# The second mixture of a two-layer decoder: rows and results scattered to their slots, tiles and results loaded plainly

## The chip, the cores and the metric

The kernel runs on one core of a Trainium2 chip. The metric is the device time of one execution in microseconds (us). Before the change three runs took 1368.06, 1368.84 and 1370.04 us; the median is 1368.84 us.

## The reference

A decoder of two layers on x of 4 x 256 tokens with 256 channels. Each layer adds three blocks to x, each on a layer norm of x: in layer 0 a recurrent mix, a cross attention to 1601 context rows and a mixture of 8 experts; in layer 1 an attention with 16 heads, a cross attention to the first 256 context rows, and a second mixture. The change is about that last block:

```python
logits = flat @ router_w.T                            # 1024 tokens x 16 experts
_, topk_idx = jax.lax.top_k(logits + router_bias, 2)
w = softmax scores of the two chosen experts, divided by their sum
for e in range(16):
    out += combine[:, e:e+1] * ((silu(flat @ Wu[e]) * (flat @ Wg[e])) @ Wd[e])
out += (silu(flat @ Su) * (flat @ Sg)) @ Sd           # shared expert
```

## The kernel before

The kernel is written engine by engine: one instruction stream each for TensorE (PE), ScalarE (ACT), the vector engine (DVE), GpSimd (POOL) and SyncE (SP), with semaphores written out by hand between them. Each engine runs its stream in order, so a wait holds all that stands behind it on that engine. Matrix products go through eight PSUM banks that are handed out in turn (`PsumBanks`): a product counts up `filled`, and the engine that reads the bank counts up `emptied`. The five phases are divided by `ended`, at which all engines meet; the second mixture is the end of phase 5.

X holds the 1024 tokens as 8 tiles of 128 tokens x 256 channels, and HN[5] their layer norm. In the second mixture every token has two choices, so there are 2048 rows of work. They are sorted by expert into slots, with each expert's count rounded up to whole tiles of 128 slots: 31 tiles (`TILES1`) always suffice. Slots without a token are padding.

1. Front. SyncE stores HN[5] to DRAM as `token_rows` (xs1, L2300 to L2303). TensorE computes the logits, the shared expert's hidden values (`shared_up`) and a count by expert (`rank1`). The vector engine picks the two experts of each token and works out the slot of each choice, `e_idx` (L1938, 128 x 16: 128 tokens, 2 choices x 8 tiles). The inverse list, the token in each slot, it makes with one-hot matrices `e_A` and `e_B` (L1942 to L1947), which TensorE multiplies (`tile_tokens`, L1085); L1954 to L1956 turn that into `e_ids`. `e_eid` (L1951) says which expert each tile has; TensorE loads it into registers. TensorE also computes the first half of the shared expert's output (`shared_down`, 4 of 8 token tiles), which the vector engine adds to X.
2. Tile loop. GpSimd gathers the rows of tile j from `token_rows` by `e_ids` (an indirect DMA of 128 rows of 1 KB, L2180), up to eight tiles ahead (`e_x` has eight buffers). TensorE turns the tile (`rows_turned`, L1094), multiplies it with the expert's up and gate weights (`tile_up`), turns the gated hidden values (`hidden_turned`) and multiplies them with the down weights (`tile_down`); the four steps of neighbouring tiles are interleaved (L1139 to L1147). ScalarE and the vector engine move and gate what lies between. ScalarE copies the result to one of four buffers `e_y` (L1453 to L1457), and SyncE stores it in slot order to DRAM as `tile_results` (ys1, L2304 to L2306).
3. Tail. TensorE computes the other half of the shared output. When all 31 stores have landed, GpSimd gathers for each token tile the rows of the first and of the second choices (L2183 to L2185, 16 indirect DMAs into `e_yg`). The vector engine works out the weights `e_w` (L1983 to L1987) and adds each weighted row tile to X (L1991, L1993), and SyncE stores X as the output (L2307 to L2309).

GpSimd's indirect DMAs are issued by its own instructions, on its own queue; SyncE's plain DMAs go to another queue.

Of the kernel before, what the change touches and what calls it, by code (L numbers as in the profile page):

```python
# [13 lines left out]
P = 128  # L14
# [72 lines left out]
def decoder(nc, x, ctx_512, L0_attn_Wk, L0_attn_Wv, L0_attn_Wr, L0_attn_Wo, L0_attn_time_decay, L0_attn_time_first,  # L87
# [5 lines left out]
    with ExitStack() as ctx:  # L93
# [5 lines left out]
        def sem(name):  # L99
            return ctx.enter_context(nc.semaphore(name))  # L100
# [209 lines left out]
        xs1 = nc.dram_tensor("token_rows_6", [B * T, C], F32, kind="Internal").ap()  # L310
        ys1 = nc.dram_tensor("tile_results_6", [TILES1 * P, C], F32, kind="Internal").ap()
# [39 lines left out]
        xs1_stored = sem("token_rows_stored")  # L351
# [9 lines left out]
        both_added = sem("both_results_added")  # L361
# [145 lines left out]
        def _(pe):  # L507
# [623 lines left out]
            tile_tokens()  # L1131
            pe.wait_ge(*banks.emptied(("sg", 1)))
            for t in range(4):
                shared_down(t)
# [13 lines left out]
            pe.wait_ge(*banks.emptied(("sg", 3)))  # L1148
            for t in range(4, NT):
                shared_down(t)  # L1150
# [4 lines left out]
        def _(act):  # L1155
# [311 lines left out]
            nc.scalar.activation(f_e[:, :, :], f_e[:, :, :], ACT.Exp).then_inc(e_exp, 1)  # L1467
            ended(act, 5)
# [3 lines left out]
        def _(dve):  # L1472
# [465 lines left out]
            link(V.tensor_copy(e_idx[:, :], slot))  # L1938
# [4 lines left out]
            V.tensor_scalar(e_A[:, :, 0, :], e_one[:, :, :], e_p, None, ALU.mult)  # L1943
            V.tensor_tensor(e_A[:, :, 1, :], e_one[:, :, :], bcast(e_high, 32), ALU.mult)
            for k in range(2):
                V.tensor_tensor(e_B[:, NT * k:NT * (k + 1), :], bcast(e_q[:, NT * k:NT * (k + 1)], P),
                                e_iota.unsqueeze(1).to_broadcast([P, NT, P]), ALU.is_equal).then_inc(onehot_ready, 1)  # L1947
            link(V.tensor_tensor(e_past[:, :, :], e_end[:, 0:E1 - 1].unsqueeze(1).to_broadcast([P, 32, E1 - 1]),
                                 bcast(e_j, E1 - 1), ALU.is_le))
            link(V.tensor_reduce(e_ef[:, :], e_past[:, :, :], AX, ALU.add))  # L1950
            V.tensor_copy(e_eid[:, :], e_ef[:, :]).then_inc(eid_ready, 1)  # L1951
# [28 lines left out]
            for t in range(4, NT):  # L1980
                residual(("sd", t), t)
# [5 lines left out]
            link(V.tensor_tensor(e_w[:, :, :], e_s[:, :, :], e_sum[:, :].unsqueeze(1).to_broadcast([P, 2, NT]), ALU.mult))  # L1987
# [10 lines left out]
        def _(pool):  # L1998
# [191 lines left out]
        def _(sp):  # L2190
# [79 lines left out]
            sp.dma_start(s_mask[:, :], mask_c).then_inc(masks_loaded, 16)  # L2270
            sp.wait_ge(*banks.filled(("a", "o", len(A_UNITS) - 1)))
# [28 lines left out]
            for g in range(2):  # L2300
                sp.wait_ge(hn_ready, NT * 5 + 4 * (g + 1))
                sp.dma_start(xs1[4 * g * P:4 * (g + 1) * P, :].rearrange("(t p) c -> p t c", p=P),
                             HN[5][:, 4 * g:4 * (g + 1), :]).then_inc(xs1_stored, 16)  # L2303
# [9 lines left out]
def shape_constants():  # L2313
# [3 lines left out]
    def angles(n, dim, base):  # L2317
# [23 lines left out]
        row(P * np.tile(np.arange(NT), 2)), row(P * np.arange(8)), row(np.tile(np.arange(NT) > 0, E1)), tri - 1], axis=1)  # L2341
# [40 lines left out]
```

## Time and profile before

| what | value |
|---|---|
| median of three runs | 1368.84 us |
| span of the profiled execution, first to last instruction | 1379.6 us |
| TensorE busy | 1272.7 us (92%) |
| vector engine busy | 868.2 us (63%) |
| GpSimd busy | 824.0 us (60%) |
| ScalarE busy | 634.6 us (46%) |
| mean granted clock of TensorE | 0.954 of full |

The profiled execution's own time is known here by its span. The profile gives, for one execution, every instruction with its start and length; times are us from the first instruction. An instruction of a shared helper has the helper's line (L515 is every matmul, L523 every turning, L1167 every ScalarE copy), so the tile names tell them apart. "PE idle before, <-X" names what released the engine.

### The profile page before, as it was taken

Reading aid. Unit: us, or ns where it says so; the run is one execution under the profiler, and the core shown is the slowest. Engines: PE = TensorE matmul, PEld = TensorE weight load, DVE = VectorE, ACT = ScalarE, POOL = GpSimd, SP = SyncE. Lnnn points to the kernel's source line nnn. Section 1 sums busy time; section 2 is a strip of 40 time slices with the busy share of each in tenths; the row PEclk is TensorE's granted clock in tenths of the full one; section 3 lists DMA queues with packets and bytes.
Section 4 is the critical chain, followed back from the end, with each engine's and each line's share of the span. In section 5 each row is a group of like instructions: output and inputs, shape, how many; then the busy total and the mean of one; then the engine's idle time right before and its main releaser. Section 6 shows DMA issues by size and latency. Waiting matters only on the chain.

```text
span 1379.6 us, 20358 instructions
## 1 busy us (share of the span) xinstructions
PE 1272.7 (92%) x7123; PEld 826.8 (60%) x7123; DVE 868.2 (63%) x1490; ACT 634.6 (46%) x1687; POOL 824.0 (60%) x748
## 2 busy tenths in 40 slices
PE   7999997999999999999999758998999999989792
PEld 4865554666666666666668643445776874556582
DVE  4756666677777777778865636675666123664443
ACT  3731123445554455544551416887665115872151
POOL 1267005799999999999993445887444004560444
PEclk9999997999999999999999888999999997998897
DMA  9501111000000000000005620000000105200263
GB/s 261 134 9 32 37 31 27 9 8 9 9 11 10 9 9 9 10 11 9 9 5 176 195 65 2 1 1 1 1 1 1 27 1 155 63 1 32 69 142 118
DMA packets 66172, 58.91 MB, mean 43 GB/s; under 512 B 19424, under 2 KB 62968, under 8 KB 65560
## 3 DMA queue, kind: packets, MB, share of 16 engines
q1 hardware_dynamic: 62952, 49.09, 12.7%
q0 software_dynamic: 3120, 8.52, 2.6%
q8 instruction: 58, 0.95, 0.3%
q14 instruction: 42, 0.34, 0.1%
HBM read 40.69 MB, written 8.52 MB: 36 GB/s over the span
## 4 chain that ended last, share of the span: by engine, by line
PE 79%; DVE 6%; ACT 5%; POOL 4%; issue 4%; DMA 1%; DVEq 0%; SPq 0%; POOLq 0%; ACTq 0%
PE PS L515 73%; PE PS L523 5%; ACT s_sc L1402 2%; POOL a_m L2137 2%; POOL a_m L2131 2%; DVE s_mx L1859 1%; ACT a_m L1356 1%; DVE pm L1622 1%; DVE HN L1504 0%; PE PS L729 0%; DMA f_xg<-token_rows,f_ids 0%; POOL s_sc L2152 0%; PE PS L685 0%; POOL f_xg L2119 0%; PE PS L623 0%
## 5 line engine op out<-in xcount | busy, mean ns | idle before, releaser
L2080 POOL TENSOR_TENSOR PWS<-PWS 128x1024 f32<-128x1024 f32 x160 | 379.7, 2373 | 45.1 <-ACT PWS L1286 25.8
L1622 DVE TENSOR_REDUCE pm<-PS 128x2 f32<-128x1024 f32 x192 | 225.8, 1218 | 69.3 <-PE PS L515 68.7
L1286 ACT ACTIVATE PWS<-PS 128x512 f32<-128x512 f32 (+1 forms) x416 | 213.3, 599 | 78.4 <-PE PS L515 78.2
L515 PE MATMUL PS<-PWS,KVR 128*64 128x256 f32 (+1 forms) x1664 | 185.8, 380 | 0.0
L515 PE MATMUL PS<-QALL,KH 128*128 128x512 f32 (+1 forms) x416 | 182.6, 439 | 0.9 <-DVE QM L1646 0.9
L515 PE MATMUL PS<-QM,KL 68*128 68x512 f32 (+1 forms) x416 | 167.3, 402 | 0.0
L2152 POOL TENSOR_SCALAR s_sc<-s_sc,s_ri 128x128 f32<-128x128 f32 (+1 forms) x256 | 104.5, 429 | 98.9 <-DVE s_ri L1866 98.9
L515 PEld LDWEIGHTS PS<-PWS,KVR 128*64 128x64 f32 (+1 forms) x1664 | 121.4, 137 | 59.0 <-issue 0.9
L515 PEld LDWEIGHTS PS<-QALL,KH 128*128 128x128 f32 (+1 forms) x416 | 77.9, 187 | 76.9 <-ACT PWS L1286 57.4
L1402 ACT ACTIVATE s_sc<-PS,s_nb 128x128 f32<-128x128 f32 (+1 forms) x256 | 104.5, 433 | 3.9 <-DVE s_nb L1862 3.9
L1859 DVE TENSOR_REDUCE s_mx<-PS 128x2 f32<-128x512 f32 (+2 forms) x112 | 65.7, 611 | 50.1 <-PE PS L515 50.0
L515 PE MATMUL PS<-KH,QALL 64*128 64x512 f32 (+1 forms) x512 | 89.3, 408 | 7.0 <-DVE pm L1622 7.0
L515 PE MATMUL PS<-a_wT,HT 128*128 128x512 f32 x192 | 93.4, 620 | 0.7 <-issue 0.7
L1297 ACT ACTIVATE QALL<-CTX 128x256 fp32r<-128x256 f32 x32 | 13.3, 417 | 154.0 <-DVE CTX L1659 154.0
L515 PEld LDWEIGHTS PS<-QM,KL 68*128 68x128 f32 (+1 forms) x416 | 79.0, 190 | 6.2
L515 PEld LDWEIGHTS PS<-KH,QALL 64*128 64x128 f32 (+1 forms) x512 | 46.9, 189 | 43.7 <-issue 26.0
L515 PE MATMUL PS<-z_HTh,z_w 128*128 128x512 f32 x192 | 67.5, 420 | 2.4 <-DVEq L502 2.4
L2180 POOL DMA_INDIRECT e_x<-token_rows,e_ids x31 | 29.5, 951 | 67.2 <-DVE e_ids L1956 46.8
L2131 POOL TENSOR_TENSOR a_m<-a_m,a_m 128x512 f32<-128x512 f32 x40 | 51.0, 1276 | 29.5 <-DVE a_m L1836 29.5
L1271 ACT ACTIVATE QALL<-PS 64x512 fp32r<-64x512 f32 x32 | 19.0, 594 | 106.3 <-PE PS L515 105.9
L1525 DVE TENSOR_TENSOR X<-X,PS 128x256 f32<-128x256 f32 x40 | 16.8, 419 | 76.8 <-PE PS L515 76.7
L1390 ACT ACTIVATE s_pt<-PS 128x512 f32<-128x512 f32 x64 | 38.5, 602 | 53.6 <-PE PS L523 53.6
(328 smaller groups left out, 2518.3 us busy)
## 6 DMA issues: line engine op xcount, KB each, us to landing
QALL<-qlo SPq DMA_DIRECT2D x32, 128.0 KB, 2.4
QM<-QALL SPq DMA_DIRECT2D x64, 64.0 KB, 2.0
f_w<-in_L_ffn_w_dram SPq DMA_DIRECT2D x2, 2048.0 KB
tile_results<-e_y SPq DMA_DIRECT2D x31, 128.0 KB
a_nat<-in_L_attn_w_qkv_dram SPq DMA_DIRECT2D x1, 3072.0 KB, 13.0
x_wq<-in_L_xattn_Wq_dram SPq DMA_DIRECT2D x1, 2048.0 KB, 10.4
x_wo<-in_L_xattn_Wo_dram SPq DMA_DIRECT2D x2, 1024.0 KB, 6.9
a_wo<-in_L_attn_w_o_dram SPq DMA_DIRECT2D x1, 2048.0 KB, 17.5
```

What stands on the lines that cost most here:

```text
L515: return nc.tensor.matmul(o, a, b, start=start, stop=stop, **kw)
L523: last = nc.tensor.transpose(ps[0:w, c:c + r], a, ident[0:r, 0:r])
L1286: nc.scalar.activation(PW[c][0:rows, j * HALF:(j + 1) * HALF], st_bank("block", LT * u + lt)[0:rows, :], ACT.Exp).then_inc(p_ready, 1)
L1390: nc.scalar.activation(s_pt[:, m % 2, 0, :], ps, ACT.Copy).then_inc(emptied["act_turned"], 1)
L1402: ins = nc.scalar.activation(s_sc[:, k % 4, h, 0:nk], ps[:, j * nk:(j + 1) * nk], ACT.Exp, bias=s_nb[:, k % 3, h:h + 1], scale=scale, accu ...
L1622: V.tensor_reduce(pm[u % 2][:, :, i // 3, i % 3], src, AX, ALU.max).then_inc(nat_read, 1)
L1859: ins = V.tensor_reduce(s_mx[:, k % 3, i * per:(i + 1) * per], banks.bank(key)[:, 0:per * nk].rearrange("p (h k) -> p h k", h=per), AX, AL ...
L2080: G.tensor_tensor(ACC[:, :], PW[0][:, :] if i == 0 else ACC[:, :], PW[i + 1][:, :], ALU.add).then_inc(acc_step, 1)
L2131: G.tensor_tensor(a_m1[:, n % 6, :], a_m1[:, n % 6, :], a_m2[:, n % 2, :], ALU.add).then_inc(m_sum, 1)
L2137: G.tensor_tensor(m1, m1, a_bt[:, i, s, :].unsqueeze(1).to_broadcast([P, 4, P]), ALU.add).then_inc(qk_ready, 1)
L2152: ins = G.tensor_scalar(s_sc[:, n % 4, h, 0:nk], s_sc[:, n % 4, h, 0:nk], s_ri[:, n % 4, h:h + 1], 1.0, ALU.mult, ALU.mult)
L2180: G.indirect_dma_start(e_x[:, j % 8, :], None, xs1, IndirectOffsetOnAxis(ap=e_ids[:, j:j + 1], axis=0)).then_inc(tile_back[j % 8], 16)
```

## The change

- Scatter ahead of the loop. `token_rows` becomes `slot_rows`, 31 x 128 rows in slot order. As soon as `e_idx` is there, GpSimd scatters HN[5] into it: 16 indirect DMAs, one for each choice and token tile. SyncE waits for all 16 and then loads tile j with a plain DMA, again up to eight tiles ahead. Padding rows have to be finite, so SyncE clears `slot_rows` early, in phase 4, with two plain DMAs from the zeroed tile `y_v`; ScalarE's first copy into `y_v` waits for these.
- Scatter in the loop. Each tile's result goes from `e_y` straight to its place by choice and token (`choice_results`): an indirect DMA on GpSimd by `e_ids`, which now counts choice and token from 1 in the matrix product, so that 0 marks padding; padding slots get rows of their own behind the 2048 (`e_dump`, `e_miss`).
- Plain loads in the tail. When all 31 scatters have landed, SyncE loads both results of each token tile in one plain DMA of 256 KB, eight in all. ScalarE weights the first result, GpSimd adds it to X, and the vector engine weights and adds the second.
- Order. The vector engine takes the shared expert's hidden values, `e_eid` and four of the adds ahead of the one-hots; TensorE computes the second half of the shared output ahead of the loop, and the vector engine adds it there.

```diff
@@ TensorE, ahead of the loop
-            tile_tokens()
             pe.wait_ge(*banks.emptied(("sg", 1)))
             for t in range(4):
                 shared_down(t)
+            tile_tokens()
+            pe.wait_ge(*banks.emptied(("sg", 3)))
+            for t in range(4, NT):
+                shared_down(t)
@@ TensorE, behind the loop
-            pe.wait_ge(*banks.emptied(("sg", 3)))
-            for t in range(4, NT):
-                shared_down(t)
@@ ScalarE, phase 4
             act.wait_ge(v_cleared, 1)
+            act.wait_ge(xs1_cleared, 32)
@@ ScalarE, tail
+            act.wait_ge(w_ready, 1)
+            for t in range(NT):
+                act.wait_ge(both_back[t], 16)
+                nc.scalar.activation(e_yg[:, t, 0, :], e_yg[:, t, 0, :], ACT.Copy, scale=e_w[:, 0, t:t + 1]).then_inc(first_weighted, 1)
@@ vector engine, front (order: e_idx, hidden(1..3), e_eid, four adds, then the one-hots)
-            link(V.tensor_copy(e_idx[:, :], slot))
+            V.tensor_copy(e_idx[:, :], slot).then_inc(idx_ready, 1)
+            for n in range(1, 4):
+                hidden(n)
...
-            V.tensor_scalar(e_A[:, :, 0, :], e_one[:, :, :], e_p, None, ALU.mult)
+            V.scalar_tensor_tensor(e_A[:, :, 0, :], e_one[:, :, :], e_p, e_one[:, :, :], ALU.mult, ALU.add)
...
+            V.tensor_scalar(e_dump[:, :], e_tiles, e_p, float(2 * B * T + 1), ALU.add, ALU.add)
...
+            link(V.scalar_tensor_tensor(e_miss[:, :], e_idf[:, :], 0.0, e_dump[:, :], ALU.is_equal, ALU.mult))
+            link(V.scalar_tensor_tensor(e_idf[:, :], e_idf[:, :], -1.0, e_miss[:, :], ALU.add, ALU.add))
             V.tensor_copy(e_ids[:, :], e_idf[:, :]).then_inc(ids_ready, 1)
@@ vector engine, tail
             for t in range(NT):
-                dve.wait_ge(*banks.emptied(("sd", t)))
-                dve.wait_ge(both_back[t], 32)
-                V.scalar_tensor_tensor(X[:, t, :], e_yg[:, t, 0, :], e_w[:, 0, t:t + 1], X[:, t, :], ALU.mult, ALU.add).then_inc(both_added, 1)
                 dve.wait_ge(both_added, t + 1)
                 V.scalar_tensor_tensor(X[:, t, :], e_yg[:, t, 1, :], e_w[:, 1, t:t + 1], X[:, t, :], ALU.mult, ALU.add).then_inc(x_final, 1)
@@ GpSimd
-            pool.wait_ge(xs1_stored, 32)
+            pool.wait_ge(xs1_cleared, 32)
+            pool.wait_ge(hn_ready, NT * 6)
+            pool.wait_ge(idx_ready, 1)
+            for t in range(NT):
+                for k in range(2):
+                    G.indirect_dma_start(xs1, IndirectOffsetOnAxis(ap=e_idx[:, k * NT + t:k * NT + t + 1], axis=0),
+                                         HN[5][:, t, :], None).then_inc(xs1_stored, 16)
             pool.wait_ge(ids_ready, 1)
             for j in range(TILES1):
-                if j >= 8:
-                    pool.wait_ge(*banks.filled(("ex", j - 8)))
-                G.indirect_dma_start(e_x[:, j % 8, :], None, xs1, IndirectOffsetOnAxis(ap=e_ids[:, j:j + 1], axis=0)).then_inc(tile_back[j % 8], 16)
-            for i in range(4):
-                pool.wait_ge(tile_sent[i], 16 * len(range(i, TILES1, 4)))
+                pool.wait_ge(*banks.emptied(("ey", j)))
+                G.indirect_dma_start(ys1, IndirectOffsetOnAxis(ap=e_ids[:, j:j + 1], axis=0),
+                                     e_y[:, j % 4, :], None).then_inc(tile_sent[j % 4], 16)
             for t in range(NT):
-                for k in range(2):
-                    G.indirect_dma_start(e_yg[:, t, k, :], None, ys1, IndirectOffsetOnAxis(ap=e_idx[:, k * NT + t:k * NT + t + 1], axis=0)).then_inc(both_back[t], 16)
+                pool.wait_ge(first_weighted, t + 1)
+                G.tensor_tensor(X[:, t, :], X[:, t, :], e_yg[:, t, 0, :], ALU.add).then_inc(both_added, 1)
@@ SyncE
+            sp.wait_ge(v_cleared, 1)
...
+            for a, z in ((0, 16), (16, TILES1)):
+                sp.dma_start(rows[:, a:z, :], zeros[:, 0:z - a, :]).then_inc(xs1_cleared, 16)
...
+            sp.wait_ge(xs1_stored, 16 * 2 * NT)
             for j in range(TILES1):
-                sp.wait_ge(*banks.emptied(("ey", j)))
-                sp.dma_start(ys1[j * P:(j + 1) * P, :], e_y[:, j % 4, :]).then_inc(tile_sent[j % 4], 16)
+                if j >= 8:
+                    sp.wait_ge(*banks.filled(("ex", j - 8)))
+                sp.dma_start(e_x[:, j % 8, :], xs1[j * P:(j + 1) * P, :]).then_inc(tile_back[j % 8], 16)
+            for i in range(4):
+                sp.wait_ge(tile_sent[i], 16 * len(range(i, TILES1, 4)))
+            for t in range(NT):
+                both = ys1[0:2 * B * T, :].rearrange("(k t p) c -> t p k c", k=2, p=P)
+                sp.dma_start(e_yg[:, t, :, :], both[t]).then_inc(both_back[t], 16)
```

## Rows read from the trace of the kernel before

**Rows 1.** The page's head: the span of the profiled execution.
```profile
span 1379.6 us, 20358 instructions
```

**Rows 2.** Timeline of the front: start, length, engine, line, operation, out<-in, count, idle before.
```profile
1278.38 0.17 DVE L1938 CAST e_idx<-e_slot 128x16 uint32<-128x16 f32 x1
1279.21 0.69 DVE L1942 TENSOR_TENSOR e_one<-e_jq,e_c 128x512 bf16<-128x512 f32 x1
1280.81 2.35 DVE L1946 TENSOR_TENSOR e_B<-e_q,e_c 128x1024 bf16<-128x1024 f32 x2
1284.80 0.18 DVE L1956 CAST e_ids<-e_idf 128x32 uint32<-128x32 f32 x1
1285.76 1.06 POOL L2180 DMA_INDIRECT e_x<-token_rows,e_ids  x1 [46.81 <-DVE e_ids L1956]
...
1289.28 0.44 PE L523 MATMUL PS<-ident,e_x 128*128 128x128 f32 x2
```

**Rows 3.** Timeline of the tile loop: TensorE's products and turnings, one ScalarE gate.
```profile
1293.14 1.06 PE L515 MATMUL PS<-m_wug,e_xT 128*128 x4
1297.90 0.28 ACT L1445 ACTIVATE e_st<-PS 128x128 f32<-128x128 f32 x1 [4.78 <-remote]
1306.45 0.64 PE L523 MATMUL PS<-ident,e_x 128*128 128x128 f32 x2
1309.56 0.38 PE L523 MATMUL PS<-ident,e_x 128*128 128x128 f32 x2
...
1346.99 0.38 PE L523 MATMUL PS<-ident,e_x 128*128 128x128 f32 x2
```

**Rows 4.** Loop by stretches: length, busy PE, PEld, DVE, ACT, POOL, clock, DMA share, GB/s.
```profile
1296.00:1303.00 7.00, 2.03 (x6) 1.10 (x5) 0.33 (x2) 0.71 (x3) 3.67 (x4) 0.73 0.35 94
1303.00:1309.00 6.00, 5.48 (x15) 4.27 (x16) 1.71 (x5) 1.95 (x8) 2.84 (x3) 0.50 0.39 112
1309.00:1348.00 39.00, 39.00 (x216) 32.92 (x215) 17.10 (x48) 19.88 (x72) 15.15 (x16) 0.99 0.58 136
```

**Rows 5.** Chain of waits, the tail: start, length, what.
```profile
1351.97 0.39 ACT e_y L1167
1352.38 1.69 DMA tile_results<-e_y
...
1354.89 0.95 POOL e_yg L2185
...
1376.43 0.48 DVE X L1991
...
1376.96 0.48 DVE X L1993
```

**Rows 6.** Timeline of the tail: GpSimd's last gather.
```profile
1373.67 0.95 POOL L2185 DMA_INDIRECT e_yg<-tile_results,e_idx  x1 [0.30 <-issue]
```

**Rows 7.** GpSimd's groups by shape: count, busy us, mean ns, idle before and releaser.
```profile
L2185 POOL DMA_INDIRECT e_yg<-tile_results,e_idx x16 | 15.2, 947 | 23.9 <-DMA tile_results<-e_y 19.3 <-issue 4.6
L2034 POOL TENSOR_TENSOR z_w<-W,z_w 128x256 fp32r<-128x256 f32 x8 | 5.9, 735 | 0.0
```

**Rows 8.** DMA issues: count, KB each, median us from issue to landing.
```profile
QM<-QALL SPq DMA_DIRECT2D x64, 64.0 KB, 2.0
m_wd<-in_L_ffn_Wd_dram SPq DMA_DIRECT2D x1, 2048.0 KB, 8.7
y_wq<-in_L_xattn_Wq_dram SPq DMA_DIRECT2D x1, 256.0 KB, 2.8
```

**Rows 9.** Timeline of the first mixture: a vector product and a gather beside it.
```profile
773.29 1.49 DVE L1791 TENSOR_TENSOR a_wT<-a_wT,a_mu 128x1280 f32<-128x1280 f32 x1
773.48 2.13 POOL L2119 DMA_INDIRECT f_xg<-token_rows,f_ids  x1 [0.30 <-issue]
```

**Rows 10.** Writers of y_v: ns min/median/max, first and last start, shapes.
```profile
L1167 ACT ACTIVATE y_v<-PS x4: 597/598/598, 1102.5 to 1105.0; 128x512 f32<-128x512 f32 x4
L2145 POOL MEMSET y_v<- x1: 3512/3512/3512, 954.1 to 954.1; 128x4096 f32 x1
```

More of the change, by code:

```diff
@@ L309, in decoder @@
         e_yg = at("e_yg", 136192, [P, NT, 2, C])
-        xs1 = nc.dram_tensor("token_rows_6", [B * T, C], F32, kind="Internal").ap()
-        ys1 = nc.dram_tensor("tile_results_6", [TILES1 * P, C], F32, kind="Internal").ap()
+        e_dump = at("e_dump", 144384, [P, 32])
+        e_miss = at("e_miss", 144512, [P, 32])
+        xs1 = nc.dram_tensor("slot_rows_6", [TILES1 * P, C], F32, kind="Internal").ap()
+        ys1 = nc.dram_tensor("choice_results_6", [(2 * NT + TILES1) * P, C], F32, kind="Internal").ap()
         filled = sem("bank_filled")
@@ L350, in decoder @@
         router_loaded = sem("router_loaded")
-        xs1_stored = sem("token_rows_stored")
+        xs1_cleared = sem("slot_rows_cleared_6")
+        xs1_stored = sem("slot_rows_stored")
+        idx_ready = sem("choice_slots_ready")
         choice_ready = sem("two_choices_ready")
@@ L360, in decoder @@
         both_back = [sem(f"both_results_loaded_{t}") for t in range(NT)]
-        both_added = sem("both_results_added")
+        both_added = sem("first_results_added")
+        first_weighted = sem("first_results_weighted")
+        w_ready = sem("choice_weights_ready")
         x_final = sem("output_rows_ready")
@@ L1937, in _ @@
             slot = e_slot[:, :, :].rearrange("p k t -> p (k t)")
-            link(V.tensor_copy(e_idx[:, :], slot))
+            V.tensor_copy(e_idx[:, :], slot).then_inc(idx_ready, 1)
+            for n in range(1, 4):
+                hidden(n)
+            link(V.tensor_tensor(e_past[:, :, :], e_end[:, 0:E1 - 1].unsqueeze(1).to_broadcast([P, 32, E1 - 1]),
+                                 bcast(e_j, E1 - 1), ALU.is_le))
+            link(V.tensor_reduce(e_ef[:, :], e_past[:, :, :], AX, ALU.add))
+            V.tensor_copy(e_eid[:, :], e_ef[:, :]).then_inc(eid_ready, 1)
+            for t in range(4):
+                residual(("sd", t), t)
+            dve.wait_ge(idx_ready, 1)
             link(V.tensor_scalar(e_qu[:, :], e_idx[:, :], P - 1, None, ALU.bitwise_and))
@@ L1947, in _ @@
                                 e_iota.unsqueeze(1).to_broadcast([P, NT, P]), ALU.is_equal).then_inc(onehot_ready, 1)
[L1948 to L1951, printed above, removed]
+            V.tensor_scalar(e_dump[:, :], e_tiles, e_p, float(2 * B * T + 1), ALU.add, ALU.add)
             ps = banks.take("ids", "dve")
@@ L1955, in _ @@
             dve.wait_ge(*banks.emptied("ids"))
+            link(V.scalar_tensor_tensor(e_miss[:, :], e_idf[:, :], 0.0, e_dump[:, :], ALU.is_equal, ALU.mult))
+            link(V.scalar_tensor_tensor(e_idf[:, :], e_idf[:, :], -1.0, e_miss[:, :], ALU.add, ALU.add))
             V.tensor_copy(e_ids[:, :], e_idf[:, :]).then_inc(ids_ready, 1)
-            for n in range(1, 4):
-                hidden(n)
-            for t in range(4):
+            for t in range(4, NT):
                 residual(("sd", t), t)
@@ L1979, in _ @@
                     gated_tile(j)
-            for t in range(4, NT):
-                residual(("sd", t), t)
             dve.wait_ge(e_exp, 2)
@@ L1986, in _ @@
             link(V.reciprocal(e_sum[:, :], e_sum[:, :]))
-            link(V.tensor_tensor(e_w[:, :, :], e_s[:, :, :], e_sum[:, :].unsqueeze(1).to_broadcast([P, 2, NT]), ALU.mult))
+            V.tensor_tensor(e_w[:, :, :], e_s[:, :, :], e_sum[:, :].unsqueeze(1).to_broadcast([P, 2, NT]), ALU.mult).then_inc(w_ready, 1)
+            dve.wait_ge(w_ready, 1)
             for t in range(NT):
-                dve.wait_ge(*banks.emptied(("sd", t)))
-                dve.wait_ge(both_back[t], 32)
-                V.scalar_tensor_tensor(X[:, t, :], e_yg[:, t, 0, :], e_w[:, 0, t:t + 1], X[:, t, :], ALU.mult, ALU.add).then_inc(both_added, 1)
                 dve.wait_ge(both_added, t + 1)
@@ L2270, in _ @@
             sp.dma_start(s_mask[:, :], mask_c).then_inc(masks_loaded, 16)
+            sp.wait_ge(v_cleared, 1)
+            zeros = y_v[:, :, :, :, :].rearrange("p b k h d -> p (b k h d)").rearrange("p (r c) -> p r c", c=C)
+            rows = xs1.rearrange("(p r) c -> p r c", p=P)
+            for a, z in ((0, 16), (16, TILES1)):
+                sp.dma_start(rows[:, a:z, :], zeros[:, 0:z - a, :]).then_inc(xs1_cleared, 16)
             sp.wait_ge(*banks.filled(("a", "o", len(A_UNITS) - 1)))
@@ L2299, in _ @@
                                  w[0, :, it * P:(it + 1) * P].rearrange("(k p) i -> p k i", p=P)).then_inc(moe1_loaded, 16)
[L2300 to L2303, printed above, removed]
+            sp.wait_ge(xs1_stored, 16 * 2 * NT)
             for j in range(TILES1):
-                sp.wait_ge(*banks.emptied(("ey", j)))
-                sp.dma_start(ys1[j * P:(j + 1) * P, :], e_y[:, j % 4, :]).then_inc(tile_sent[j % 4], 16)
+                if j >= 8:
[6 more added lines that the diff above has]
+                sp.dma_start(e_yg[:, t, :, :], both[t]).then_inc(both_back[t], 16)
             for t in range(NT):
@@ L2340, in shape_constants @@
         tri, row(np.arange(P)), row(P * np.arange(32)), row(np.arange(32)), np.arange(P, dtype=f)[:, None],
-        row(P * np.tile(np.arange(NT), 2)), row(P * np.arange(8)), row(np.tile(np.arange(NT) > 0, E1)), tri - 1], axis=1)
+        row(P * np.arange(2 * NT)), row(P * np.arange(8)), row(np.tile(np.arange(NT) > 0, E1)), tri - 1], axis=1)
     a = angles(T, P, 1000000.0)
```

## The prediction

> **What bounds the kernel now.** I read the page first: span 1379.6 us [rows 1]. The runs' median is 1368.84 us, 10.8 below that span, so the profiled execution holds at least 10.8 us that a run doesn't have; this matters below. Then I read the chain of waits over the last stage, which is all that the change touches on the path, and its timeline engine by engine. The stage has three parts.
>
> Front: the token slots e_idx are written at 1278.55; the ids of the tiles' tokens (e_ids) follow at 1284.98, GpSimd starts the first gather at 1285.76 (0.78 after its release), and TensorE turns tile 0 at 1289.28 [rows 2].
>
> Loop: between tile 7 (1309.56) and tile 30 (1346.99) TensorE is busy for all of the stretch at clock 0.99, a tile every 37.43 / 23 = 1.63 us [rows 3, 4]. GpSimd's gathers hide in it. Tiles 0 to 30 would take 30 x 1.63 = 48.8 us at that pace but take 57.7: 8.9 us are lost before tile 7. There TensorE's matmul of 1293.14 ends by the records at 1294.20, yet ScalarE is released by it only at 1297.90 [rows 3]; TensorE works 2.03 of the 7 us after 1296, and then runs at clock 0.50 [rows 4], where tile 6 to tile 7 takes 3.11 us [rows 3].
>
> Tail: the last result tile's store begins at 1352.38 and takes 1.69; GpSimd starts its 16 gathers at 1354.89 and the last one at 1373.67, so they end at 1374.62; the vector engine's last pair of adds runs from 1376.43 to 1377.44, and the last output row lands with the span's end, 2.1 us later [rows 1, 5, 6]. The tail is bound by GpSimd: 0.947 us an indirect DMA and 4.6 / 15 = 0.30 between two [rows 7]. All 27.2 us after 1352.38 are exposed.
>
> **The change part by part.** In short, 31 gathers hidden in the loop and 16 exposed ones in the tail become 16 scatters ahead of the loop and 31 scatters hidden in it. So I work out the new start of the loop, then the new tail.
>
> *Start of the loop.* GpSimd now waits for e_idx: 1278.55 + 0.78 = 1279.33. Sixteen indirect DMAs at 0.947 + 0.30 follow: the last starts 15 x 1.25 = 18.8 later and ends at 1299.1. No scatter is in the trace; I price one as a gather [rows 7]. SyncE waits for all 16, so the last landing counts: 1.8 us (from the last gather's end, 1374.62, to the add at 1376.43 [rows 5, 6]). Then SyncE loads tile 0 with a plain DMA: 2.0, the median of the 64 KB ones [rows 8]; the 128 KB store's 1.69 [rows 5] and the 256 KB load's 2.8 [rows 8] bound it. Tile 0 is turned at 1302.9 in place of 1289.28: +13.6. The loads that follow fit: eight are in flight and each has 1.63 us.
>
> *Stretched scatters.* In the first mixture a gather that started at 773.48 took 2.13 us while the vector engine multiplied two SBUF operands until 774.78; it ended 0.83 after that [rows 9]. In the new order the vector engine makes the one-hots while GpSimd scatters. Before, that group ran from 1279.21 to 1283.16, 3.95 us almost without a break [rows 2]; one of its operations takes a second operand now. Cost between 0 (each scatter starts in a gap) and 4.3 (all of it waited for). I take 1.5: the group lasts about three scatters, each held for some half of an operation (1.18 us in the long e_B ones, less in others).
> The Trainium skill, in "SBUF — State Buffer", section "Who interferes with whom", states this as a lock: a vector instruction with two SBUF inputs keeps out a GpSimd instruction that reads SBUF. The 2.13 us row agrees. By that rule GpSimd's adds in the tail and the vector engine's, both with two SBUF inputs, would take turns too; that would put the tail's pace at the sum of the two below, 1.22 us a tile of rows.
>
> *TensorE's clock.* Before, TensorE was at full clock when the loop began. Now it has nothing between the shared products and tile 0, about 3 to 6 us, and a wait of that kind was followed by 0.50 [rows 4]. At half clock a tile costs 3.11 - 1.63 = 1.5 more [rows 3]. Bounds 0 and 4.5 (three tiles); I take 2.
>
> *Tail.* GpSimd's scatters need 1.25 a tile and the last four result tiles come faster than that, so the last scatter starts about 1 us after its tile is ready: 1352.4 + 1.1 + 0.95 = 1354.4; landed 1.8 later, 1356.2. SyncE then issues eight loads of 256 KB: the first lands after 2.8 at most, I take 2.5: 1358.7 [rows 8]. 2 MB took 8.7 us to land [rows 8], so they come some 0.9 us apart. ScalarE weights one in about 0.45 (an estimate from its 0.39 for a tile of that size [rows 5]); GpSimd adds 128x256 in 0.735 [rows 7]; the vector engine's add takes 0.48 [rows 5]. The pace lies between 0.9 (loads alone) and 1.22 (the two adds in turn); I take 1.1. Last GpSimd add: 1359.2 + 0.74 + 7 x 1.1 = 1367.6; vector engine 1368.2; stored 2.1 later, 1370.3. Against 1379.6 that is -9.3; bounds -11.3 (0.9 a tile, faster landings) and -6 (1.22 a tile, scatters that land 2 us later).
>
> *At nothing.* Clearing the scattered rows moves 31 x 128 KB; at 2048 KB in 8.7 us [rows 8] some 17 us, between the clearing of y_v at 957.6 and ScalarE's first copy into it at 1102.5 [rows 10], which now waits for it. Without that cover it would delay ScalarE by what is left; 145 us are there. On SyncE it stands ahead of the latent weights' loads, which wait for later work anyway. The second half of the shared products and their four adds leave the tail, where the gathers hid them, for the front, where the scatters hide them: ids at about 1295, shared products until 1297 (1301 at half clock), tile 0 at 1304. The added small vector operations (dump rows, misses) lie there too: ids are first needed by tile 0's scatter, after 1306. If the shared products came later than tile 0, the excess would be paid in full. Result buffers: four at 1.63 give 6.5 us; copy, scatter and landing need about 0.4 + 0.3 + 0.95 + 1.8 = 3.5. On SyncE the output stores queue behind the eight loads; the last store does not feel it.
>
> *Sum.* +13.6 + 1.5 + 2.0 - 9.3 = +7.8 us. I count the lost 8.9 us as belonging to the profiled execution: they are one event, and the span exceeds the runs by more. So 7.8 goes on the median: 1368.84 + 7.8 = 1376.6.
>
> **Rivals.**
> 1. *The 8.9 us are in the runs too, and go with the gathers.* For it: the event falls while GpSimd issues gathers without a pause, which the new loop doesn't do. Against: the same gathers run through the rest of the loop without it, and the runs are 10.8 shorter than the span. Then +7.8 - 8.9 = -1.1: 1367.7, not slower. It decides once the runs hold over 7.8 us of that loss. With this the tail's better end gives 1365.7.
> 2. *Scatters cost what the held gathers cost.* If all 16 were issued at some 1.7 us, as stretched ones, the start moves by 16 x 0.45 = 7.2, less the 1.5 already counted: 1382.3. Only a few meet two-operand work, hence against.
> 3. *Scatters land late and the four result buffers bind the loop.* From landings above 4.9 us each further us costs 31 / 4 = 7.8 us. At 6 us: +8.5, so 1385. The trace has no landing that slow beside plain 1 KB rows in this stage.
> 4. *Cheap front:* break-even needs 16 scatters to take 7.8 less, 0.76 us each. No indirect DMA here is under 0.94 + 0.30.
>
> **How the numbers follow.** Forecast 0.60, rival 1 0.24, rival 2 0.08, rival 3 0.05, rival 4 0.03. The forecast's own range, from the bounds (least 13.3 + 0 + 0 - 11.3 = +2.0, most 14.4 + 4.3 + 4.5 - 6 = +17.2, seldom all at once), is 1371 to 1383. A difference under 0.2% (2.7 us) can't be told from none here. Forecast: 0.57 slower, 0.03 within. Rival 1 spreads over 0.10 faster, 0.10 within, 0.04 slower. Rivals 2 and 3: slower; rival 4: faster. Together, with a little more for faster because a scatter's price is untested: 0.15, 0.14, 0.71. The range takes in rival 1 and rival 2: 1364 to 1384.
>
> **What would show it.** Right: 16 indirect DMAs on GpSimd from about 1279 to 1300, one or a few of them above 1.2 us under the one-hots; tile 0 turned 13 to 16 us later after e_idx than before; 1.63 us a tile from then on, with a first stretch at clock 0.5; under 19 us from the last result tile to the end. Wrong: a scatter clearly shorter than 0.95 or longer than 1.3 without two-operand work, a loop slower than 1.63 with ScalarE waiting for sent results, or a before whose runs contain the lost 8.9 us.

## The result, and the profile after

The changed kernel takes 1372.55 us in the median of 18 runs, the kernel before 1368.11 us in the median of the 18 beside them. The ratio on record is 1.0053, 95% interval 1.0035 to 1.0071: slower by 0.53%, 7.2 us (4.8 to 9.7). It is not the ratio of the two medians, which lie 4.4 us apart. The prediction was +7.8, and 1376.6 us, which is 4.1 above the measured median. Runs of one kernel spread over 13 to 15 us, so what follows goes by the trace where it can, and from e_idx on: e_idx was written at 1271.70 here and at 1278.55 before [rows 2], and those 6.85 us are put down to that spread: the change moves nothing on TensorE or the vector engine ahead of e_idx, and nine executions with the changed front had it anywhere from 1269.2 to 1278.0.

The page of the changed kernel:

```profile
span 1370.6 us, 20372 instructions
```

Timeline of its front (start, length, engine, line, operation, idle before), against [rows 2]:

```profile
1271.53 0.17 DVE L1949 CAST e_idx<-e_slot 128x16 uint32<-128x16 f32 x1
1272.54 1.11 POOL L2194 DMA_INDIRECT slot_rows<-HN,e_idx  x1 [38.09 <-DVE e_idx L1949]
...
1283.36 2.35 DVE L1966 TENSOR_TENSOR e_B<-e_q,e_c 128x1024 bf16<-128x1024 f32 x2
1284.57 1.97 POOL L2194 DMA_INDIRECT slot_rows<-HN,e_idx  x1 [0.30 <-issue]
...
1293.15 0.96 POOL L2194 DMA_INDIRECT slot_rows<-HN,e_idx  x1 [0.30 <-issue]
1295.57 7.72 SPq L2327 DMA_DIRECT2D e_x<-slot_rows  x12
1297.68 1.13 PE L529 MATMUL PS<-ident,e_x 128*128 128x128 f32 x4 [6.78 <-DMA e_x<-slot_rows]
```

Sixteen scatters run from 0.84 us after e_idx to 1294.11; the loads start 1.46 later, and tile 0 is turned 2.11 after that: 25.98 us after e_idx's end (1271.70) in place of 10.73. Groups of the new work (count, busy us, mean ns of one, idle before), against [rows 7]:

```profile
L2199 POOL DMA_INDIRECT choice_results<-e_y,e_ids x31 | 29.7, 959 | 30.1 <-ACT e_y L1173 29.2 <-issue 0.9
L2194 POOL DMA_INDIRECT slot_rows<-HN,e_idx x16 | 17.0, 1063 | 42.7 <-DVE e_idx L1949 38.1 <-issue 4.6
L2203 POOL TENSOR_TENSOR X<-X,e_yg 128x256 f32<-128x256 f32 x8 | 6.3, 804 | 5.9 <-ACT e_yg L1478 5.9
L2007 DVE SCALAR_TENSOR_TENSOR X<-e_yg,e_w,X 128x256 f32<-128x256 f32 x8 | 5.3, 706 | 6.5 <-POOL X L2203 6.5
L1478 ACT ACTIVATE e_yg<-e_yg,e_w 128x256 f32<-128x256 f32 x8 | 4.1, 508 | 7.6 <-DMA e_yg<-choice_results 7.6
```

A scatter costs what a gather cost: 0.96 where nothing stretches it, against 0.947. Stretches of the loop and of the tail (length, busy PE, PEld, DVE, ACT, POOL, clock, DMA share, GB/s), against [rows 4]:

```profile
1295.00:1302.00 7.00, 4.16 (x12) 3.04 (x13) 1.46 (x4) 0.28 (x1) 0.00 (x0) 0.51 0.60 183
1302.00:1309.00 7.00, 7.00 (x40) 5.95 (x39) 2.76 (x9) 3.21 (x13) 2.62 (x3) 1.00 0.41 126
1309.00:1348.00 39.00, 39.00 (x218) 32.95 (x216) 17.07 (x48) 19.85 (x73) 22.89 (x25) 1.00 0.43 138
...
1357.50:1365.00 7.50, 0.00 (x0) 0.00 (x0) 3.48 (x6) 3.95 (x8) 5.12 (x7) 0.50 0.97 316
```

The clock is 0.51 as the loop begins, and from 1302 TensorE is busy without a break; tile 30 is turned at 1346.50, 48.82 after tile 0. The tail's timeline, against [rows 5]:

```profile
1351.47 0.38 ACT L1173 ACTIVATE e_y<-PS 128x256 f32<-128x256 f32 x1 [0.26 <-PE PS L521]
1352.98 0.96 POOL L2199 DMA_INDIRECT choice_results<-e_y,e_ids  x1 [0.30 <-issue]
1355.53 3.96 SPq L2332 DMA_DIRECT2D e_yg<-choice_results  x8
1358.23 0.51 ACT L1478 ACTIVATE e_yg<-e_yg,e_w 128x256 f32<-128x256 f32 x1 [4.75 <-DMA e_yg<-choice_results]
1361.07 2.31 POOL L2203 TENSOR_TENSOR X<-X,e_yg 128x256 f32<-128x256 f32 x3 [0.34 <-ACT e_yg L1478]
1361.87 2.19 DVE L2007 SCALAR_TENSOR_TENSOR X<-e_yg,e_w,X 128x256 f32<-128x256 f32 x3 [0.62 <-POOL X L2203]
...
1364.68 2.19 DVE L2007 SCALAR_TENSOR_TENSOR X<-e_yg,e_w,X 128x256 f32<-128x256 f32 x3 [0.62 <-POOL X L2203]
```

Three adds of the two engines, taken singly out of these:

```profile
1361.79 0.73 POOL L2203 TENSOR_TENSOR X<-X,e_yg 128x256 f32<-128x256 f32 x1
1361.87 0.93 DVE L2007 SCALAR_TENSOR_TENSOR X<-e_yg,e_w,X 128x256 f32<-128x256 f32 x1 [0.62 <-POOL X L2203]
1362.51 0.87 POOL L2203 TENSOR_TENSOR X<-X,e_yg 128x256 f32<-128x256 f32 x1
```

From the last result tile (1351.85) to the end it is 18.8 us in place of 27.2: the DMA engines are full (share 0.97) while loads and output stores run, and the last add ends at 1366.87. But the program ends 3.8 us after that, and the end is not the last store's. At the end of a phase TensorE, ScalarE, the vector engine and GpSimd each run a drain instruction (L508) and then wait until the drains of all four are over. The trace's records of the engines' end, after their last work:

```
SyncE: last wait over, the stores have landed       1368.72
GpSimd: last add                                    1365.29 to 1366.19
GpSimd: drain (L508, at the end of the phase)       1365.15 to 1370.11
ScalarE, vector engine, TensorE: wait for it over   1370.14
```

### The profile page after: what moved, and what is told of

Same layout as the page of the kernel before. It is cut to its first block, busy times and chain, and to the rows that moved or that the text cites. A ratio compares the mean times of both kernels' runs of the same rounds, so it can differ in the third digit from the quotient of the medians.

```text
span 1370.6 us, 20372 instructions
## 1 busy us (share of the span) xinstructions
PE 1266.1 (92%) x7123; PEld 825.0 (60%) x7123; DVE 866.1 (63%) x1485; ACT 638.3 (47%) x1695; POOL 831.3 (61%) x756
## 4 chain that ended last, share of the span: by engine, by line
PE 79%; POOL 6%; DVE 5%; ACT 5%; issue 2%; DMA 2%; SPq 0%; DVEq 0%; POOLq 0%; ACTq 0%
PE PS L521 73%; PE PS L529 5%; ACT s_sc L1408 2%; POOL a_m L2151 2%; POOL a_m L2145 2%; DVE s_mx L1870 1%; POOL slot_rows L2194 1%; ACT a_m L1362 1%; DVE pm L1633 1%; DVE HN L1515 0%; PE PS L735 0%; DMA f_xg<-token_rows,f_ids 0%; POOL s_sc L2166 0%; DMA e_yg<-choice_results 0%; PE PS L691 0%
## 5 line engine op out<-in xcount | busy, mean ns | idle before, releaser
L1666 DVE RECIPROCAL PS<-PS 128x256 f32<-128x256 f32 x32 | 55.9, 1747 | 6.3 <-PE PS L521 6.3
## 6 DMA issues: line engine op xcount, KB each, us to landing
x_wq<-in_L_xattn_Wq_dram SPq DMA_DIRECT2D x1, 2048.0 KB, 10.8
```

The lines of the kernel that those rows point to most:

```text
L1666: V.reciprocal(sums, sums).then_inc(inv_ready, 1)
```

## The experiments

All times in the table are worked out from rows of each run's trace: from e_idx's end to the turning of tile 0, from there to tile 30, and from the last result tile to the end of the span (tile 30 to the last result tile is 5.36 in all). These three numbers come from one execution each; the tail of the changed kernel, left as it is, took 18.4 to 19.4 in five of them. The ratio is that of the runs to the kernel before on the same chip.

| kernel | to tile 0 | tiles 0 to 30 | tail | ratio (95%) |
|---|---|---|---|---|
| before | 10.73 | 57.71 | 27.22 | 1 |
| before, a second execution | 10.63 | 47.59 | 27.21 | |
| changed | 25.98 | 48.82 | 18.78 | 1.0053 (1.0035 to 1.0071) |
| new front, old tail | 25.85 | 48.83 | 27.30 | 1.0130 (1.0090 to 1.0169) |
| 12 scatters | 20.86 | 47.14 | 18.40 | 1.0022 (0.9995 to 1.0049) |
| 28 products more | 32.81 | 47.08 | 18.58 | 1.0116 (1.0085 to 1.0147) |
| 11 products more | 25.90 | 47.14 | 19.36 | 1.0023 (0.9993 to 1.0053) |
| one-hots three times | 26.94 | 47.14 | 19.11 | |
| tail on the vector engine | 25.92 | 48.83 | 16.55 | 1.0055 (1.0029 to 1.0080) |
| GpSimd adds four tiles | 25.95 | 48.99 | 17.52 | |
| tail on the vector engine, 11 products | 25.89 | 48.68 | 19.24 | 1.0056 (1.0031 to 1.0081) |

**The kernel before again: were the 8.9 us in its runs?** No edit.

> The kernel before once more, for a second profiled execution. Theory (the 8.9 us lost in the loop are an event of one execution): tile 0 turned 10.7 us after e_idx again, tile 0 to tile 30 in 47 to 49 us, TensorE without a stretch of late products; from the last result tile to the end 27.2. Rival (they come with the gathers, in every execution): tile 0 to tile 30 in 55 to 58 us again.

Its timeline, then two stretches in the columns of [rows 4]:

```profile
1277.90 0.17 DVE L1938 CAST e_idx<-e_slot 128x16 uint32<-128x16 f32 x1
...
1288.70 0.38 PE L523 MATMUL PS<-ident,e_x 128*128 128x128 f32 x2
...
1336.29 0.27 PE L523 MATMUL PS<-ident,e_x 128*128 128x128 f32 x1
...
1295.00:1302.00 7.00, 7.00 (x40) 5.85 (x39) 2.85 (x8) 3.55 (x14) 5.17 (x7) 1.00 0.64 176
1302.00:1336.00 34.00, 34.00 (x190) 28.72 (x189) 14.96 (x42) 17.19 (x64) 16.67 (x18) 1.00 0.75 156
```

Where [rows 4] has 2.03 us of TensorE in 7, here it is 7.00, under the same gathers. The event belongs to one execution, whose span of 1379.6 is also above the longest of the 18 runs, 1373.61; it cost 57.71 - 47.59 = 10.1 us with the half clock behind it. What brought it stays open.

**The new front with the old tail.** Results are stored plainly by slot and gathered behind the loop; both adds are on the vector engine.

```diff
-            for j in range(TILES1):
-                pool.wait_ge(*banks.emptied(("ey", j)))
-                G.indirect_dma_start(ys1, IndirectOffsetOnAxis(ap=e_ids[:, j:j + 1], axis=0),
-                                     e_y[:, j % 4, :], None).then_inc(tile_sent[j % 4], 16)
+            for i in range(4):
+                pool.wait_ge(tile_sent[i], 16 * len(range(i, TILES1, 4)))
...
+            for t in range(NT):
+                for k in range(2):
+                    G.indirect_dma_start(e_yg[:, t, k, :], None, ys1, IndirectOffsetOnAxis(ap=e_idx[:, k * NT + t:k * NT + t + 1], axis=0)).then_inc(both_back[t], 16)
...
@@ SyncE, between the loads of tiles
+                if j >= 10:
+                    result_stored(j - 10)
...
```

> The changed front (16 scatters, plain tile loads, the order of work) with the tail of the kernel before: results stored plainly by slot, 16 gathers behind the loop, both adds on the vector engine. Theory (front dear, tail cheap, the late products of the loop not in the runs): the front costs 15.3 us and the loop nothing, so 15 to 16.5 us over the kernel before (ratio 1.011 to 1.012), and 8 to 9.5 us over the changed kernel; from the last result tile to the end 27 us. Rival (the 8.9 us that the profiled loop before lost are in its runs and go with the gathers): 6 to 7 us over the kernel before (ratio 1.005), and the new tail then gains nothing.

```profile
1269.80 0.17 DVE L1945 CAST e_idx<-e_slot 128x16 uint32<-128x16 f32 x1
...
1295.83 0.47 PE L529 MATMUL PS<-ident,e_x 128*128 128x128 f32 x1 [6.71 <-DMA e_x<-slot_rows]
```

The front's price (25.85) and the old tail's (27.30) stand side by side, and the ratio 1.0130 is 17.7 us (12.3 to 23.0): the rival's 6 to 7 us are outside. Against the changed kernel the trace gives 8.5 us more, the tail's gain.

**Twelve scatters instead of 16** (the second choices of token tiles 4 to 7 are left out, their rows stay zero).

```diff
-                for k in range(2):
+                for k in range(2 if t < 4 else 1):
...
-            sp.wait_ge(xs1_stored, 16 * 2 * NT)
+            sp.wait_ge(xs1_stored, 16 * 12)
```

> The changed kernel without four of its 16 scatters ahead of the loop (the second choices of token tiles 4 to 7; their rows stay zero). Theory (issue on GpSimd sets the loop's start, 0.96 + 0.30 us each): tile 0 is turned 5.0 us sooner after e_idx, at 20.9 in place of 26.0, and the run is 5 us shorter than the changed kernel, ratio to the kernel before 1.0010 to 1.0025. Rival (landing, the loads or the shared products set the start): less than 2 us shorter than the changed kernel.

```profile
1269.77 0.17 DVE L1949 CAST e_idx<-e_slot 128x16 uint32<-128x16 f32 x1
...
1286.36 0.96 POOL L2194 DMA_INDIRECT slot_rows<-HN,e_idx  x1 [0.30 <-issue]
...
1290.80 0.44 PE L529 MATMUL PS<-ident,e_x 128*128 128x128 f32 x2 [1.70 <-DMA e_x<-slot_rows]
```

25.98 - 20.86 = 5.12 us for four: 1.28 each, so the issue on GpSimd sets the start. The loop is 1.7 shorter too, which I had not expected: the wait ahead of tile 0 is 1.70 in place of 6.78, and the clock stays full.

**TensorE kept busy ahead of tile 0**, first with 28 products, then with 11.

```diff
+                if j == 0:
+                    ps = begin(("ex", 0), "dve")
+                    for n in range(28):
+                        mm(ps[:, C:2 * C], HT[5][:, 0, 0:P], HT[5][:, 1, 0:C])
...
```

> The changed kernel with 28 more products of 128x128 by 128x256 on TensorE between the shared products and tile 0, into an unused half of tile 0's bank, so that TensorE doesn't idle while the scatters end. Theory (the loop's start at half clock costs something): clock near full at tile 0; tile 0 to tile 30 takes 47 to 48 us in place of 48.8, and the run is 1 to 2 us shorter than the changed kernel. Rival (what the half clock costs is hidden behind the vector engine's and ScalarE's part of the first tiles): tile 0 to tile 30 takes 48.6 to 49 and the run is the same within 0.5 us.

Two stretches of the run with 28, columns as in [rows 4]:

```profile
1291.00:1302.00 11.00, 11.00 (x53) 9.70 (x52) 0.00 (x0) 0.00 (x0) 0.96 (x1) 1.00 0.39 121
1302.00:1309.00 7.00, 6.62 (x38) 5.47 (x37) 2.95 (x9) 2.00 (x9) 0.49 (x1) 1.00 0.30 87
```

I had sized them badly: 12.25 us of products held tile 0 back by 6.8 us, and the run is longer, not shorter. What it shows all the same is the loop at full clock: 47.08, 1.74 less. The second try, with `range(11)`:

> The changed kernel with 11 more products on TensorE ahead of tile 0, which take 4.8 us by the run with 28 (56 records in 12.25 us) and so end before tile 0's rows land. Theory: tile 0 at 26.0 after e_idx as in the changed kernel, at full clock, tile 0 to tile 30 in 47.1 us as in the run with 28 in place of 48.8, so 1.7 us shorter than the changed kernel: ratio to the kernel before about 1.004. Rival (the shorter loop of the run with 28 came from rows that had all landed by then, not from the clock): 48.8 again.

```profile
1292.43 6.55 PE L521 MATMUL PS<-m_wd,e_hs 128*128 128x256 f32 x16
1298.82 4.91 PE L521 MATMUL PS<-HT 128*128 128x256 f32 x22
1303.86 0.94 PE L529 MATMUL PS<-ident,e_x 128*128 128x128 f32 x4
```

Tile 0 came at 25.90 and the loop took 47.14, so the shorter loop is the clock's and not that of rows landed early. That the products filled the wait to the last 0.13 us was in part chance: the shared products ahead of them took 6.55 us here, at a granted clock of 0.50 from 1292 to 1297, where those of the changed kernel took 4.71. In the runs it is 1.0023, about 4 us below the changed kernel, with an interval that overlaps its.

**The one-hots e_B made three times over.**

```diff
+            for again in range(2):
+                for k in range(2):
+                    ins = V.tensor_tensor(e_B[:, NT * k:NT * (k + 1), :], bcast(e_q[:, NT * k:NT * (k + 1)], P),
+                                          e_iota.unsqueeze(1).to_broadcast([P, NT, P]), ALU.is_equal)
+                link(ins)
```

> The changed kernel with the two one-hot operations e_B made three times over, so that some 7 us of them lie beside the scatters in place of 2.4. Theory (a GpSimd scatter is held while the vector engine works on two SBUF operands): three or four scatters of 1.7 to 2.1 us in place of one, tile 0 turned 28 to 29 us after e_idx in place of 26.0. Rival (the one long scatter of 1.97 us under e_B was chance, or its DMA's): still one or two long ones, tile 0 at 25.5 to 26.5.

```profile
1282.24 4.75 DVE L1967 TENSOR_TENSOR e_B<-e_q,e_c 128x1024 bf16<-128x1024 f32 x4
...
1283.38 1.22 DVE L1967 TENSOR_TENSOR e_B<-e_q,e_c 128x1024 bf16<-128x1024 f32 x1
...
1287.03 2.37 DVE L1971 TENSOR_TENSOR e_B<-e_q,e_c 128x1024 bf16<-128x1024 f32 x2
...
1283.47 1.97 POOL L2199 DMA_INDIRECT slot_rows<-HN,e_idx  x1 [0.30 <-issue]
1285.74 0.96 POOL L2199 DMA_INDIRECT slot_rows<-HN,e_idx  x1 [0.30 <-issue]
1287.01 0.96 POOL L2199 DMA_INDIRECT slot_rows<-HN,e_idx  x1 [0.31 <-issue]
1288.27 1.97 POOL L2199 DMA_INDIRECT slot_rows<-HN,e_idx  x1 [0.30 <-issue]
```

Two long scatters instead of one, tile 0 at 26.94: more than the rival's, less than my 28, and the number of long ones is the rival's. What speaks for the theory is where they end. The line of 1283.38 is the second of the four operations by itself. The scatter of 1283.47 began just behind its start and ended 0.84 after its end (1284.60); [rows 9] had 0.83, and the four stretched scatters of the changed kernel had 0.83 and 0.84. Those of 1285.74 and 1287.01 began within 0.12 us of an operation's end and cost nothing more. So a scatter waits for the operation that runs as it starts, and how many are hit depends on where they fall. The other way round nothing shows: an operation e_B that began under a running scatter took 1.22 us, as one without a scatter did.

**The tail without ScalarE and GpSimd**, whose own loops over the token tiles go.

```diff
             for t in range(NT):
+                dve.wait_ge(both_back[t], 16)
+                V.scalar_tensor_tensor(X[:, t, :], e_yg[:, t, 0, :], e_w[:, 0, t:t + 1], X[:, t, :], ALU.mult, ALU.add).then_inc(both_added, 1)
                 dve.wait_ge(both_added, t + 1)
```

> The changed kernel, but both results are weighted and added on the vector engine, as before; ScalarE and GpSimd take no part in the tail. Theory (the tail is paced by its eight loads, which with the output stores keep the DMA engines full from 1357.5 to 1365): within 1 us of the changed kernel, ratio to the kernel before 1.0045 to 1.0060; a pair of adds 1.05 us, eight of them 8.5, as long as the loads. Rival (adds on two engines hold each other up, 1.22 us a tile): taking GpSimd's away makes it 1.5 to 2.5 us shorter than the changed kernel. Second rival (splitting the adds is what shortened the tail): 3 us or more longer.

The adds' groups, and a stretch of the tail:

```profile
L2005 DVE SCALAR_TENSOR_TENSOR X<-e_yg,e_w,X 128x256 f32<-128x256 f32 x8 | 3.9, 485 | 0.3
L2003 DVE SCALAR_TENSOR_TENSOR X<-e_yg,e_w,X 128x256 f32<-128x256 f32 x8 | 3.9, 482 | 3.7 <-DMA e_yg<-choice_results 3.7
...
1355.00:1361.50 6.50, 0.00 (x0) 0.00 (x0) 5.15 (x12) 0.00 (x0) 0.00 (x0) 0.50 0.94 311
```

The tail is 2.2 us shorter, 16.55: as much as the first rival had said, but for another reason in the main. The last add ended 14.42 after the last result tile in place of 15.01, which is 0.6; the loads pace both (0.94 and 0.97 of the DMA engines). From the last add to the end it is 2.13 in place of 3.76, which is 1.6: GpSimd's drain was over at 1355.27, 3.90 after its last scatter, and SyncE ends the program. This is one execution, and in the runs the gain is not to be seen (1.0055); their interval, 3.5 us to either side, would hide it.

Then the changed kernel with ScalarE's and GpSimd's loops cut to four token tiles; the vector engine adds both for the rest:

```diff
-            for t in range(NT):
+            for t in range(4):
                 pool.wait_ge(first_weighted, t + 1)
...
+                if t >= 4:
+                    dve.wait_ge(both_back[t], 16)
+                    V.scalar_tensor_tensor(X[:, t, :], e_yg[:, t, 0, :], e_w[:, 0, t:t + 1], X[:, t, :], ALU.mult, ALU.add).then_inc(both_added, 1)
                 dve.wait_ge(both_added, t + 1)
```

> The changed kernel, with ScalarE and GpSimd taking the first results of token tiles 0 to 3 only; the vector engine adds both for tiles 4 to 7. Theory (the changed kernel's end waits for GpSimd's drain, 3.9 us after its last add): GpSimd is through 3 us sooner, its drain ends before the last row is stored, and SyncE ends the program; tail 16.3 to 17.2 in place of 18.8. Rival (the drain takes what is left until the DMAs have landed, whenever it starts): it still ends 1 us or more after SyncE's last wait, tail 18 or more.

GpSimd's drain ended 2.55 us ahead of the end, and the end is SyncE's again: 17.52, 0.3 above what I had expected, 1.3 below the changed kernel.

**Both savings together**: the edit with 11 products and that of the tail on the vector engine.

> The changed kernel with both adds of the tail on the vector engine and 11 more products ahead of tile 0. Theory (the two savings stand in different stages and add): tile 0 at 26.0 after e_idx, loop 47.1, tail 16.6, so 3.8 us shorter than the changed kernel, ratio to the kernel before 1.001 to 1.004, still not below it, since the front's 15.3 us stand against 10.6 in the tail and half a us in the loop. Rival (they do not add, since the DMA engines or the last stores bound the end): tail 18 or more.

Neither came through in this execution. One stretch of it:

```profile
1295.00:1302.00 7.00, 6.49 (x27) 5.03 (x28) 2.38 (x7) 1.26 (x6) 0.00 (x0) 0.76 0.67 200
```

The 11 products left a wait of 2.01 us, and the clock fell once the loop had begun: 48.68. The last add ended at 1364.50, but the last packets of the output stores ended from 1367.1 to 1367.7, up to 1.9 us behind the others; an instruction fetch of 16 KB lies between (1365.73 to 1367.02). Whether it held them is not shown. In the runs it is 1.0056, and no version of the change was shown to be faster than the kernel before; the nearest that does all of the work, with 11 products alone, can't be told from it (0.9993 to 1.0053).

**A shorter front for the kernel before.** The front had turned out to be the dear part, so I looked at what precedes e_idx: e_any was ready at 1271.18, and TensorE's count by expert came 3.4 us later, behind three shared products. First the count was moved, and on the vector engine the first of the hidden values behind e_ids:

```diff
-            for i, n in ((0, 0), (1, 0), (0, 1)):
-                shared_up(i, n)
+            shared_up(0, 0)
             rank1()
-            for i, n in ((1, 1), (0, 2), (1, 2), (0, 3), (1, 3)):
+            for i, n in ((1, 0), (0, 1), (1, 1), (0, 2), (1, 2), (0, 3), (1, 3)):
...
```

> The kernel before, with its gathers and its tail, but TensorE counts by expert (rank1) after the first of the shared expert's products instead of after three of them, and the vector engine takes the first hidden values behind e_ids. In the profile of before e_any was ready 3.4 us ahead of that count. Theory (the path to the loop runs through e_idx in either kernel): e_idx, tile 0 and the end all come 2.5 to 3.4 us sooner, ratio 0.9975 to 0.9982. Rival (the shared products or the weights hold the loop): e_idx sooner, tile 0 not, ratio 1.000.

The rival was right: ratio 0.9995 (0.9960 to 1.0030). e_ids now came 9.6 us after e_idx, since tile_tokens waited for the shared products. So these were moved too: tile_tokens ahead of the last two, and the shared down products behind the loop.

```diff
-            for i, n in ((1, 1), (0, 2), (1, 2), (0, 3), (1, 3)):
+            for i, n in ((1, 0), (0, 1), (1, 1), (0, 2), (1, 2)):
                 shared_up(i, n)
             tile_tokens()
-            pe.wait_ge(*banks.emptied(("sg", 1)))
-            for t in range(4):
-                shared_down(t)
+            for i, n in ((0, 3), (1, 3)):
+                shared_up(i, n)
...
```

> The kernel before (gathers, plain stores, its tail) with a shorter front: count by expert after the first shared product, tile_tokens ahead of the last two, the down products of the shared expert and their adds all behind the loop, under the tail's gathers. The run with the early count alone had e_idx 4.1 us after e_any, but tile_tokens waited for seven shared products. Theory: ids 6.4 after e_idx again, tile 0 10.7 after e_idx, so 14.9 us after e_any in place of 18.1 before; loop 47.2 to 48, tail 27.3; 3 us shorter than the kernel before, ratio about 0.998. Rival (the 16 down products and eight adds do not fit under the gathers): tail over 28.5 us, the gain is lost.

Tile 0 came 14.7 after e_any, the tail took 27.39, but the loop 48.82: ratio 0.9981 (0.9959 to 1.0002). With one down product, and its add, back ahead of the loop:

```diff
             for i, n in ((0, 3), (1, 3)):
                 shared_up(i, n)
+            pe.wait_ge(*banks.emptied(("sg", 1)))
+            shared_down(0)
...
```

> The short front with one down product of the shared expert back ahead of the loop, in the 1.35 us in which TensorE waited for tile 0's rows. In the run with the short front tile 0 came 14.7 us after e_any in place of 18.1, but the clock fell to half 1.5 us into the loop and tiles 0 to 30 took 48.8 in place of 47.2 to 47.6. Theory (the wait ahead of tile 0 brought the fall): tile 0 again 14.7 after e_any, full clock through the loop, 47.2, so 3 to 4 us shorter than the kernel before, ratio 0.997 to 0.998. Rival (the fall has another cause, such as the thin work of the first tiles): half clock and 48.5 to 49 again, ratio 0.998 to 0.999.

The stretch at the loop's start without and with that product, of the two runs:

```profile
1275.00:1282.00 7.00, 6.63 (x27) 5.16 (x28) 2.40 (x7) 1.44 (x6) 5.17 (x7) 0.76 0.36 104
```
```profile
1279.00:1286.00 7.00, 6.72 (x35) 5.13 (x36) 3.13 (x9) 2.00 (x9) 5.17 (x7) 1.00 0.41 116
```

Full clock, tiles 0 to 30 in 47.42, and 0.9956 (0.9933 to 0.9979), 6 us: faster than the kernel before. The trace accounts for 3.3 of these (18.1 - 14.8 from e_any to tile 0), or 2.7 against the 17.6 of the second execution of before; the rest lies within the interval, whose near end is 2.9 us. The intervals with and without the one product overlap, so what that product gives is shown by the two traces alone.

## Why the prediction was right

The sum was +13.6 + 1.5 + 2.0 - 9.3. Against the second execution of the kernel before, the changed one has:

- *Start of the loop and stretched scatters, +15.1 forecast.* 25.98 - 10.63 = +15.35. Sixteen scatters took 17.0 us, 16 x 0.96 = 15.4 and 1.6 of stretching (forecast 1.5): 1.0 of it in one scatter under e_B, 0.3 under e_past. The landing was shorter than forecast (1.46 for 1.8), the first wait 0.06 longer. The run with 12 scatters shows the price of one, the run with three times the one-hots what stretches them. The Trainium skill, "SBUF — State Buffer", section "Who interferes with whom", has this as a lock between a vector instruction with two SBUF inputs and a GpSimd instruction that reads SBUF: the scatters that end 0.83 to 0.84 after the operation under which they began agree.
- *The clock, +2.0.* 48.82 - 47.59 = +1.2, or 1.7 against the loops at full clock behind the same front (47.08 to 47.14). The place was right, the size somewhat too large. What decides whether the clock falls is open: with a wait of 1.70 and of 1.97 us ahead of tile 0 it stayed full, with 1.35 and 2.01 in two other runs it fell.
- *The tail, -9.3.* 18.78 - 27.21 = -8.4. Two errors lie in it. The adds came sooner than forecast: the last vector add ended 15.0 us after the last result tile, not 15.8, since GpSimd's adds came (1366.19 - 1359.55) / 7 = 0.95 us apart, as the loads landed (ScalarE waited for a load before each of its eight), and not 1.1. The adds do take turns, but a turn is cheaper than forecast. In the three adds shown singly above, the vector add began under a GpSimd add and ended 0.28 after its end (1362.52, 1362.80); the next GpSimd add began under the vector add and ended 0.58 after that (1363.38). In the six traces in which GpSimd adds, all 26 vector adds that began under a GpSimd add ended 0.28 after it, and 18 of the 20 GpSimd adds that began under a vector add 0.58 to 0.59 after that. So a pair in turn takes 0.28 + 0.58 = 0.86 us, less than the loads' 0.95, and not 1.22, the sum of what each takes alone; the means of 0.804 (0.735 in [rows 7]) and 0.706 (0.48) are waits for the other engine. And "stored 2.1 later" was wrong: it is 3.76, because GpSimd's drain ends 3.92 after its last add. Before, it ended 3.90 after the last gather, at 1378.51, and SyncE's last wait at 1379.19 covered it; an engine that is done early hides its drain, and the change took the last work to GpSimd.
- *At nothing.* The two DMAs that clear the rows were issued from 960.2 on and landed within 10.8 us; ScalarE's first copy into y_v came at 1105.0. The shared products were through at 1290.9, 6.8 ahead of tile 0. Neither shows on the path, as forecast. Result buffers never held ScalarE.
- *The 8.9 us.* They were left out as one execution's event; the second execution has none, and the new front with the old tail is slower by far more than rival 1 allowed.

Together +15.35 + 1.2 - 8.4 = +8.2 by the trace, +7.2 (4.8 to 9.7) by the runs. That the sum came so near is in part luck: the clock was priced 0.8 too high and the tail's gain 0.9 too high, and in the tail the adds that came sooner and the end that came later cancel in part. In short: 16 indirect DMAs were moved from the tail, where they took 19.7 us, to the front, where they take 21.6 and start the loop 15 us later; the tail gave back only 8.4, since a DMA of 2 MB, its adds and a drain took the gathers' place.

## What to carry to other kernels

Moving a serial string of indirect DMAs from one end of a loop to the other gains only what it finds as cover there; count the landing, the plain loads and the adds that follow as new serial work. Read a profiled stall against a second execution before you price it. Where two engines hold each other up, look at how long one ends after the other, and don't add what each takes alone. Look at which engine's drain ends the program: a last short instruction on GpSimd may cost more than its length.

## What was not expected of the hardware

- GpSimd's drain ended 3.90 us after its last instruction in the kernel before and in the tail on the vector engine (an indirect DMA), and 3.92 in the changed kernel (an add, 12 us after the last indirect DMA); with 12 scatters it was 3.59, with the new front and the old tail 3.12. In the phases ahead drains ended 0.05 to 0.93 us after the last instruction. What takes the time is open.
- e_idx was written between 1269.2 and 1278.0 in nine executions of kernels with the changed front, which are alike up to there; so much of the spread of the runs arises ahead of the stage.
